# Weighing and adding the gathered expert rows on GpSimd in three operations a body, in place of eight on VectorE

## The reference

```python
x = x + 0.5 * L0_ffn(layernorm(x))   # 8 experts, the best 2 of each token, weighted sum
x = x + L0_attn(layernorm(x))        # 16 heads of 8 channels over 512 tokens
...
out = jnp.sum(out * weights[..., None], axis=1)   # in L0_ffn: two rows of experts, weighed
```

## Time and profile before

| | |
|---|---|
| times of three runs | 1391.99, 1392.63, 1400.24 us (median 1392.63) |
| the profiled execution | 1398.67 us, its span 1396.9 us |
| busy over the span | PE 1236.2, DVE 1123.6, ACT 876.3, POOL 513.5 us |
| TensorE's granted clock, mean | 0.953 of full speed |
| attention | about 295 to 704 us of the span |

### The profile page before, as it was taken

One profiled execution on the slowest core, in us unless ns is written; L12 is line 12 of the kernel. 1 busy time (PEld: TensorE's weight loads), 2 busy tenths in 40 slices (PEclk: granted clock), 3 DMA queues, 4 the chain that ended last, 5 costly groups with the idle time before them and its releaser, 6 DMA issues.

```text
span 1396.9 us, 22511 instructions
## 1 busy us (share of the span) xinstructions
PE 1236.2 (88%) x7168; PEld 783.7 (56%) x7168; DVE 1123.6 (80%) x2387; ACT 876.3 (63%) x1535; POOL 513.5 (37%) x762
## 2 busy tenths in 40 slices
PE   6768999678899879988888999899999899899998
PEld 5657989312222212322277999866666356666665
DVE  6865979789988989898677989877876787778785
ACT  5855777358887868877887777633333588333442
POOL 6772337543543506520363236605330320210100
PEclk9988999679998989999999999999999999999999
DMA  7495556522212202210253566456363010253534
GB/s 267 131 357 179 204 203 227 159 70 79 90 48 84 86 26 96 89 44 13 78 225 126 188 222 217 139 113 142 84 130 70 11 42 19 52 121 73 116 69 121
DMA packets 116608, 167.94 MB, mean 120 GB/s; under 512 B 18884, under 2 KB 63460, under 8 KB 115468
## 3 DMA queue, kind: packets, MB, share of 16 engines
q1 hardware_dynamic: 109324, 151.82, 36.7%
q0 software_dynamic: 7168, 14.69, 3.6%
HBM read 80.72 MB, written 45.09 MB: 90 GB/s over the span
## 4 chain that ended last, share of the span: by engine, by line
PE 53%; DVE 25%; issue 8%; ACT 7%; DMA 4%; POOL 2%; SPq 1%; DVEq 0%; ACTq 0%; POOLq 0%
PE bank L1678 6%; DVE shared L2297 6%; PE bank L2375 5%; PE pair L950 4%; PE pair L952 4%; PE pair L951 4%; PE pair L2357 3%; PE pair L1590 3%; PE pair L1592 3%; PE pair L1591 3%; PE pair L2289 3%; DVE shared L1034 3%; DMA shared<-p_coef_rows 2%; ACT shared L2365 2%; DVE shared L1032 2%
## 5 line engine op out<-in xcount | busy, mean ns | idle before, releaser
L2297 DVE TENSOR_REDUCE shared<-pair 128x2 f32<-128x1024 f32 x256 | 309.8, 1217 | 40.7 <-PE pair L2289 37.8
L2365 ACT ACTIVATE shared<-pair 128x1024 f32<-128x1024 f32 x256 | 260.5, 1021 | 51.1 <-PE pair L2357 49.5
L950 PE MATMUL pair<-shared 128*128 128x256 f32 (+1 forms) x704 | 228.0, 324 | 7.1 <-issue 3.6
L951 PE MATMUL pair<-shared 128*128 128x256 f32 (+1 forms) x704 | 218.2, 310 | 0.0
L952 PE MATMUL pair<-shared 128*128 128x256 f32 (+1 forms) x704 | 218.0, 310 | 0.0
L1034 DVE TENSOR_TENSOR shared<-shared 128x512 fp32r<-128x512 f32 x208 | 155.7, 757 | 59.9 <-ACT shared L1024 56.7
L1645 ACT ACTIVATE shared<-pair 128x512 f32<-128x512 f32 x144 | 85.7, 595 | 180.9 <-PE pair L1592 180.8
L1590 PE MATMUL pair<-shared 128*128 128x512 f32 x288 | 154.6, 537 | 4.9 <-DVE shared L1600 4.9
L1018 ACT ACTIVATE shared<-pair,shared 128x256 f32<-128x256 f32 x288 | 121.3, 476 | 49.9 <-PE pair L952 43.5
L950 PEld LDWEIGHTS pair<-shared 128*128 128x128 f32 x704 | 137.8, 196 | 14.9 <-issue 4.5
L2375 PE MATMUL bank<-shared 128*9 128x512 f32 x1024 | 138.8, 615 | 4.5 <-ACT shared L2365 4.3
(11 more groups left out here) (384 smaller groups left out, 2253.4 us busy)
## 6 DMA issues: line engine op xcount, KB each, us to landing
shared<-shared SPq DMA_DIRECT2D x144, 256.0 KB
shared<-p_coef_rows SPq DMA_DIRECT2D x64, 512.0 KB, 6.4
shared<-xs_rows SPq DMA_DIRECT2D x36, 256.0 KB, 3.0
ys_rows<-shared SPq DMA_DIRECT2D x36, 256.0 KB
w_keep<-shared SPq DMA_DIRECT2D x8, 1024.0 KB, 12.2
shared<-w_keep SPq DMA_DIRECT2D x16, 512.0 KB
shared<-p_q_parts SPq DMA_DIRECT2D x64, 96.0 KB, 2.3
shared<-p_k_parts SPq DMA_DIRECT2D x64, 96.0 KB, 2.4
```

What stands on the lines that cost most here:

```text
L950: nc.tensor.matmul(out_bank, w_hi, x_hi, start=start, stop=False)
L951: nc.tensor.matmul(out_bank, w_hi, x_lo, start=False, stop=False)
L2297: nc.vector.tensor_reduce(mneg[:, i, 2 * c:2 * c + 2], pair_of("max", b, m)[:], AX_X, ALU.max, negate=True).then_inc(s["mx_read"], 1)
L2365: nc.scalar.activation(probs[st % 2][:, 2 * p:2 * p + 2, :], pair_of("exp", b, 2 * st + p)[:], ACT.Exp, scale=scale).then_inc(s["exp_done" ...
```

## The change

VectorE's eight pieces a body are gone from bodies 0 to 4 (`combine_piece` is no longer called there; other phases still use it). GpSimd does the same sums in three operations a body: step 0 multiplies the eight gathered tiles (128x1024) in place with the weights, which are read as a broadcast; step 1 adds the first row of each token to `x_res` (128x512), step 2 the second. Step 0 stands in `pool_b` between fetch 3 and `xbo_pool`, steps 1 and 2 between `seq_root` and fetch 4. Step 1 waits for step 0 and step 2 for step 1 on a semaphore.

```diff
--- before.py
+++ after.py
@@ -329,6 +329,26 @@
                                                   in1=x_res[:, t, :], op0=ALU.mult, op1=ALU.add)
             if i == TILES - 1:
                 done.then_inc(x_mix, 1)
+
+        CONSTS = 9
+
+        def combine_pool(g, occ, b, step, done):
+
+            ts = slice(b * TILES, (b + 1) * TILES)
+            rows = staged[b % 2][:].rearrange("p k (i e) -> p (k i) e", e=E)
+            if step == 0:
+                per = B // 2 - 1 + b % 2
+                g.wait_ge(gathered[b % 2], 16 * 2 * TILES * (per * occ + b // 2 + b % 2))
+                w = w_tok[:, ts, :].rearrange("p i k -> p (i k)").unsqueeze(2).to_broadcast([P, 2 * TILES, E])
+                g.tensor_tensor(rows, rows, w, ALU.mult).then_inc(x_mix, 1)
+                return
+            pair = rows.rearrange("p (i k) e -> p i k e", k=2)
+            if step == 1:
+                g.wait_ge(x_mix, 2 * (B * occ + b) + 1)
+                g.tensor_tensor(x_res[:, ts, :], pair[:, :, 0, :], x_res[:, ts, :], ALU.add).then_inc(pool_chain, 1)
+                return
+            g.wait_ge(pool_chain, done)
+            g.tensor_tensor(x_res[:, ts, :], pair[:, :, 1, :], x_res[:, ts, :], ALU.add).then_inc(x_mix, 1)
 
         def route_consts(g):
 
@@ -2555,8 +2575,6 @@
                 if b + FIRST < B and at == 18:
                     v_dve(v, b + FIRST, bank[7])
                 if b + AHEAD < B:
-                    if at in COMBINE_AT:
-                        combine_piece(v, occ0, b + AHEAD, COMBINE_AT.index(at))
                     if at == 24:
                         norm_stats(v, f0 + b + AHEAD, b + AHEAD)
                     if at == 25:
@@ -2567,8 +2585,6 @@
                         pick_dense(v, routes)
                     if routes and b == B - 1 and st == 15:
                         weights_dense(v, routes)
-
-            COMBINE_AT = (13, 15, 16, 17, 19, 20, 21, 23)
 
             def dve_b(v, b, par, first_, last_):
                 for st in range(STEPS):
@@ -2616,9 +2632,14 @@
                 fetch((0, 1), (1, 4), (2, 6))
                 msplit_pool(g, b, 2)
                 fetch((3, 9))
+                if b + AHEAD < B:
+                    combine_pool(g, occ0, b + AHEAD, 0, 0)
                 xbo_pool(b)
                 if routes is not None and b:
                     seq_root(g, routes, b - 1)
+                if b + AHEAD < B:
+                    combine_pool(g, occ0, b + AHEAD, 1, 0)
+                    combine_pool(g, occ0, b + AHEAD, 2, CONSTS + b + 1)
                 fetch((4, 12))
                 if b + FIRST < B:
                     split_pool(g, "q", b + FIRST)
```

## The result

The changed kernel takes 1402.16 us at the median of 13 runs (1398.52 to 1408.29), the kernel before 1392.85 on the same occasions. The ratio is 1.0059, interval [1.0042, 1.0077], so the change costs 8.2 us (5.8 to 10.7); the two medians by themselves lie 9.3 us apart. Executions that were disturbed as a whole, one of before at 2772 us among them, are left out of every ratio. The forecast was +2.8 us. The profiled execution of the changed kernel took 1398.54 us, near the lower end of its own runs, and that of before 1398.67, 6 us above its median; so the two spans (1396.7 and 1396.9) must not be compared. Stretches of them can.

What follows compares the result with a forecast made beforehand. It took a chain of waits through VectorE, partly TensorE, to bound the attention bodies; body 0 -1.5, bodies 1 to 3 +3.6, body 4 +0.7 gave +2.8 on 1392.63, so 1395.4 us; range 1387 to 1403.

Steps and rivals of the forecast that it cites:

- the forecast proper: Whole kernel: slower by +0 to +6 us, centre +2.8, chance 0.60.
- Durations of steps 1 and 2, and their start: GpSimd's two adds: 1.27 us each, starting when the root ends; the skill's figure would give 1.12 each.
- Step 0 hidden before L2422: GpSimd's multiplication after fetch 3: 2.45 us fits into 2.84 us of idle time before `xbo_pool`, costing nothing.
- Turn 3 at 16.15 after the z update: Bodies 1 to 3: TensorE begins maxima turn 3 at 16.15 us instead of 13.63, waiting for GpSimd's split.
- What the pieces' removal gives back: Bodies 1 to 3: without VectorE's pieces TensorE gains 1.25 us by the T transpose.
- Net +1.2 in each of bodies 1 to 3: Stall of +2.52 us at turn 3, -1.25 by T, 0.1 caught up: +1.2 each, +3.6 together.
- Body 0, -1.5: First attention body: VectorE's piece no longer stands still beside GpSimd, saving 1.13 at turn 3 and perhaps 0.4 at k.
- Body 4, +0.7: Last changed body: L626 held for 1.25 us, less gains of 0.18 and 0.35; turn 3 not held.
- the lock on L626: Body 4: VectorE's two-input routing operation stands still beside GpSimd's step 0 for 1.25 us; otherwise the sum is 1.25 less.
- the clock rival: TensorE's new pauses may shift, remove or add a low-clock stretch: 1388 or 1402 us, chance 0.10 down, 0.10 up.
- GpSimd at half the rate: Rival: broadcast or interleaved rows make the three GpSimd operations twice as long; +19 us, 1411.5 us, chance 0.08.
- The change does not do what it says: Rival: same sums on another engine, but pieces stay elsewhere; no time of its own, no chance given.

Runs made afterwards that it cites:

- none: Kernel before with the combine of the five bodies left out, expert rows fetched but neither weighed nor added; 1389.40 us, ratio 0.9958.
- warm: Changed kernel with 14 useless TensorE transposes ahead of maxima turn 3 in bodies 1 to 3; 1393.67 us, ratio 1.0011.
- delay: Kernel before, pieces kept on VectorE, GpSimd's add L2422 run two more times after the root in bodies 1 to 3; 1398.97 us, ratio 1.0056.
- half: Changed kernel with only step 2 moved behind maxima split 3, step 1 staying before fetch 4; 1392.50 us, ratio 0.9986.
- late: Changed kernel with steps 1 and 2 moved behind maxima split 3 on GpSimd's queue; 1388.30 us, ratio 0.9965.
- late2: The changed kernel with steps 1 and 2 behind maxima split 3, timed a second time; 1388.49 us, ratio 0.9956.

## Why the prediction was right, and where it was short

The time lies in the range, the sign is right, "within 1%" came true, and the mechanism is the one that was named: the queue of GpSimd in front of split 3. The size was off: +8.2 against +2.8, outside the +0 to +6 of the forecast proper. That the range held it is in part luck, since 1402.16 lies 0.8 us below its upper end and the second timing, 1404.73, lies above it.

- *Durations of steps 1 and 2, and their start*: 1.26 and 1.27 us measured, 1.27 taken. Right; the other estimate, 1.12, was too low.
- *Step 0 hidden before L2422*: right. Its length was 1.91, not 2.45; it made no difference there.
- *Turn 3 at 16.15 after the z update*: measured 16.08. Right. Releaser L2345 as named.
- *What the pieces' removal gives back*: -1.25 by the T turn; none against before shows 1.35 for the whole body. Right.
- *Net +1.2 in each of bodies 1 to 3*: +1.12 at full clock (warm, bodies 1 and 2). Right. In body 3 before and warm both have low stretches, so there the +1.12 is taken over and not measured.
- *Body 0, -1.5*: the rows of fetch 3, in the timelines of before and after, give it.

```profile
304.91 0.98 POOL L281 DMA_INDIRECT staged<-ys_rows,slots  x1
```

```profile
302.40 0.98 POOL L281 DMA_INDIRECT staged<-ys_rows,slots  x1
```

  From there to the z update of body 1 it was 52.47 us and is 50.65: -1.8. The piece that had stood still beside GpSimd's split is gone, and TensorE waits 0.40 us before turn 3 in place of 1.53.
- *Body 4, +0.7*: the lock on L626 was priced at 1.25 us and was 0.5: step 0 took 1.90 us and not 2.45, and it held the operation until 518.12. From its z update to the next, 48.93 us fell to 48.31. So body 4 came out near -0.1. That turn 3 would not be held there was right.
- *The step that was mis-sized*: "+1.2 each" was forecast as the whole effect of a 2.5 us pause, and the clock was left to a rival, at one chance in ten each way, as something that "may shift, remove or add" a stretch. It is a term of the sum, with a sign. In the profiled execution it measures 2.50, 1.56 and 2.6 us (53.30 and 52.36 against warm's 50.80; 63.78 against 61.21 from body 3 to 4, where routing work is mixed in), 6.6 us in all. With it the sum reads -1.8 + 3 x 1.12 - 0.1 + 6.6 = +8.1 us, against 8.2 measured. Without it the sum reads +1.5, and warm measured a ratio of 1.0011, which is +1.5 us.
- *How far this sum can be trusted*: not to the tenth. It takes the kernel before as free of low stretches in body 2. Its profiled execution wasn't: from fetch 3 of body 0 to the z update of body 5 that one took 265.47 us and the changed kernel's 268.40, only 2.9 more, because before lost 3.9 us in body 2 to a low stretch of its own (53.62 against 49.68). That execution was 6 us above before's median, so such a stretch is probably not in most of its executions; no trace shows it. And the changed kernel's second timing lost 10.6 us (7.1 to 14.1).
- *What the rows had shown*: the prediction read the low stretches of before as coming "after long runs at 2.4". In that trace the stretch from 496 us on stands right behind TensorE's longest pause of body 3, 2.57 us (its line is further up), and the one from 514 on behind a pause of 2.22. A new pause of 2.5 us or more was therefore more likely to add a stretch than to remove one. The stretch of body 2 lies behind a wait of only 1.27 us, before T at 427.50, and bodies 1 and 3 had the same wait and no low stretch; for that one the cause stays open.
- *The range* held the time because the clock rival, which named 1402 for its bad case, had widened it upward to +10, not because the centre was near.
- *GpSimd at half the rate*: did not happen. *The change does not do what it says*: it does.

## What to carry to other kernels

When work goes to an engine that looks idle, read that engine's queue at the place where it is put, up to the next thing that somebody waits for. GpSimd was busy 37% of the time, and yet there was no slack at all between the root and split 3, and 2.7 us of adds there cost TensorE 2.5; the same adds 7 us later cost nothing in bodies 1 to 3 and turned a loss of 0.6% into a gain of 0.4%. A pause of TensorE has to be priced at its length plus what a lower clock behind it costs; here the three pauses cost 3 x 2.47 = 7.4 us by themselves (warm against none), of which the missing pieces gave 4 us back, and the low clock 6.6 on top.

## What the runs showed of the hardware

- A pause of 2.96 us in an otherwise busy stretch was followed by TensorE's lower clock in all six cases (three bodies, two executions), for 3 to 7 us, and cost 1.5 to 2.7 us a time. One of 2.87 us (delay) was followed by it in one body and not in the two others. Pauses of 1.64 us (half), in three bodies, were not. Useless transposes in the pause kept the clock up.
- Length alone does not decide it. The pause of 2.56 to 2.58 us late in body 3, which every kernel of this case has, was followed by the lower clock within 2 us in nine of the ten traces, and in delay it was not. Waits of 1.55 us (delay, body 0) and 1.76 (late and late2, body 4) were followed by it, and waits as long at the same operations in before and in warm were not.
- GpSimd's multiplication of 1024 float32 elements by a weight that is the same over each 128 (a broadcast operand) took 1.91 us, while its add of 512 to 512 took 1.27. Twice 1.27 would be 2.5. Whether the operand that stands still or the operation makes the difference was not tried.
- A VectorE operation of 128x8 elements with two SBUF inputs stood still beside one of GpSimd's (0.67 us in place of 0.16), as the 128x128 pieces had in the earlier trace rows. The Trainium skill, "SBUF — State Buffer", section "Who interferes with whom", says this of such pairs and names no size below which it would not hold, and the trace agrees. The reduces of the maxima, which read PSUM, kept their 1.22 us beside all of it.
